# A macaron network of Mamba, mixture-of-experts and attention layers on one core: the plus one of the convolved channels' gate, made by ScalarE in place of VectorE

## The reference

```
zxbcdt = x @ in_w
z   = zxbcdt[..., :256]
xBC = zxbcdt[..., 256:256 + 512]
xp  = jnp.pad(xBC, ((0, 0), (3, 0), (0, 0)))
xBC = sum(xp[:, k:k + T, :] * conv_w[:, k] for k in range(4)) + conv_b
xBC = jax.nn.silu(xBC)
xs, Bm, Cm = xBC[..., :256], xBC[..., 256:384], xBC[..., 384:]
y = _ssd(xs * dt[..., None], dt * A, Bm, Cm)      # a scan over chunks with a carried state
y = (y + D_skip * xs) * jax.nn.silu(z)
y = y * rsqrt(mean(y * y) + 1e-05) * norm_w
return y @ out_w                                   # summed over experts with routing weights
```

## Time and profile before

| | |
|---|---|
| median of 3 runs | 2091.86 us (2088.32 to 2097.05) |
| the profiled execution | 2089.54 us, span 2087.8 us |
| mean granted TensorE clock | 0.883 |
| busy: TensorE, VectorE, ScalarE, GpSimd | 1661.6, 1350.3, 864.6, 1048.5 us |
| start of L1698, first and last of 64 | 310.2 and 982.7 us |
| L1704, 64 times | 67.6 us |
| L1809, 58 times, first and last start | 389.1 and 993.6 us |

### The profile page before, as it was taken

The page is one execution under the profiler, slowest core; times in us unless marked ns, Lnnn a source line. Parts: engine busy times, 40 slices in busy tenths (PEclk is TensorE's granted clock), DMA queues, the critical chain, the costliest instruction groups (busy, mean ns, idle before and its releaser), DMA issues. The chain is left out here.

```text
span 2087.8 us, 37246 instructions
## 1 busy us (share of the span) xinstructions
PE 1661.6 (80%) x11038; PEld 1393.8 (67%) x11039; DVE 1350.3 (65%) x3003; ACT 864.6 (41%) x1914; POOL 1048.5 (50%) x1188
## 2 busy tenths in 40 slices
PE   6889954899999999999978899528992786377773
PEld 4569941688888888888855698417881565277662
DVE  4535457899999999999655344574663565733435
ACT  2212226455555555555422122125661464334331
POOL 2135532577777777777621355244434551456552
PEclk9989956899999999999979899559995898588876
DMA  6001130000000000000050011502211410011114
GB/s 217 1 23 36 38 85 0 1 1 1 1 1 1 1 1 1 1 1 1 1 177 1 22 35 37 178 8 55 60 51 33 126 41 21 12 38 39 38 36 138
DMA packets 68555, 81.59 MB, mean 39 GB/s; under 512 B 25488, under 2 KB 40752, under 8 KB 68416
## 3 DMA queue, kind: packets, MB, share of 16 engines
q1 hardware_dynamic: 54432, 51.46, 8.0%
q0 software_dynamic: 13856, 28.40, 5.0%
q10 hardware_dynamic: 128, 0.02, 0.0%
HBM read 54.93 MB, written 24.90 MB: 38 GB/s over the span
## 5 line engine op out<-in xcount | busy, mean ns | idle before, releaser
L869 PE MATMUL ps<-w,inner_slot 128*128 x1760 | 258.7, 292 | 62.2 <-DVE y L960 37.9
L869 PEld LDWEIGHTS ps<-w,inner_slot 128*128 128x128 f32 x1760 | 229.3, 203 | 78.4 <-issue 77.6
L857 PE MATMUL ps<-gT,w_slot 128*128 128x128 f32 x1760 | 257.6, 294 | 22.9 <-ACT gT L891 19.1
L857 PEld LDWEIGHTS ps<-gT,w_slot 128*128 128x128 f32 x1760 | 235.0, 208 | 32.7 <-issue 21.3
L822 POOL DMA_INDIRECT y_rows<-y,slot_row x149 | 150.1, 1007 | 204.6 <-DVE y L954 108.0
L816 POOL DMA_INDIRECT rows_in<-xn_rows,slot_token x188 | 187.7, 998 | 125.4 <-PE ps L845 74.3
L1804 DVE SCALAR_TENSOR_TENSOR cv<-ps,cw,cv 128x1021 f32<-128x1021 f32 (+2 forms) x192 | 245.0, 1276 | 8.5 <-ACT cv L1698 5.9
L937 DVE TENSOR_TENSOR hb<-ps,b 128x512 f32<-128x512 f32 x142 | 98.2, 691 | 201.3 <-PE ps L857 116.1
L1976 POOL TENSOR_TENSOR y<-t,sz 128x256 f32<-128x256 f32 x128 | 94.4, 738 | 185.6 <-DVE t L1848 182.7
L1575 PE MATMUL ps<-xnT,win 128*128 128x512 f32 x256 | 128.7, 628 | 29.6 <-DVE cv L1804 26.2
L1624 PE MATMUL ps<-XB,LM 128*128 128x64 f32 x1024 | 142.5, 262 | 0.0
(11 more groups left out here) (298 smaller groups left out, 4201.6 us busy)
## 6 DMA issues: line engine op xcount, KB each, us to landing
w<-in_L_ffn_W SPq DMA_DIRECT2D x6, 2048.0 KB, 10.5
back<-y_rows SPq DMA_DIRECT2D x32, 256.0 KB, 5.3
xn_rows<-xn SPq DMA_DIRECT2D x24, 256.0 KB
y_rows<-y SPq DMA_DIRECT2D x71, 64.0 KB, 1.5
rows_in<-xn_rows,slot_token POOLq DMA_INDIRECT x220
y_rows<-y,slot_row POOLq DMA_INDIRECT x149
xn_rows<-rows SPq DMA_DIRECT2D x8, 256.0 KB
out_x<-x SPq DMA_DIRECT2D x8, 256.0 KB, 3.4
```

The costliest lines, as they stand in the source:

```text
L857: ins = nc.tensor.matmul(h1[:, u, b * P:(b + 1) * P], w[:, b * P:(b + 1) * P], k.gT[:, r, :], start=True, stop=True)
L869: ins = nc.tensor.matmul(py[:, q % 2, :], k.inner_slot[:, q % RING, b * P:(b + 1) * P], w_dn[:, ds(e * (FB * D) + b * D, D)], start=(b == ...
```

## The change

For the pieces inside the loop ScalarE makes the plus one too. `early_gate` is renamed `twice_sigmoid` and is called in the loop in place of `tanh_piece`; VectorE's function and its call go. The semaphores, their counts and who waits for them stay, except that ScalarE now waits for its own tanh ahead of the Identity. GpSimd's product waits for `sigmoid` as before.

```
 # ScalarE's queue
-            def early_gate(n):
+            def twice_sigmoid(n):
                 tanh_piece(n)
                 wait(act, a["tanh"], n + 1)
                 inc(A.activation(th[:, :], th[:, :], ACT.Identity, bias=k.ones[:, 0:1]), a["sigmoid"])
...
                 if ok(t - CLOSE):
                     close_unit(t - CLOSE)
                 if piece_of(t, 2) is not None:
-                    tanh_piece(piece_of(t, 2))
+                    twice_sigmoid(piece_of(t, 2))
                 if ok(t - 1):
                     square(t - 1)
...
 # VectorE's queue
-            def twice_sigmoid(n):
-                wait(dve, a["tanh"], n + 1)
-                inc(V.tensor_scalar(th[:, :], th[:, :], 1.0, None, ALU.add), a["sigmoid"])
...
                 if piece_of(t, 1) is not None:
                     tap(piece_of(t, 1), 1)
-                if piece_of(t, 2) is not None:
-                    twice_sigmoid(piece_of(t, 2))
```

More of the change, by code:

```diff
@@ L1750, in _ @@
             do(A.activation(q[:, :], u_[:, :], ACT.Ln))
-            early_gate(0)
+            twice_sigmoid(0)
             inc(A.copy(m.pickA[:, :, :], bcast(sel[:, 0, :], 2, P)), picked)
-            early_gate(1)
+            twice_sigmoid(1)
             begin(2)
@@ L1758, in _ @@
             do(A.activation(m.cd[:, :], ps_tot, ACT.Exp))
-            early_gate(2)
+            twice_sigmoid(2)
             begin(3)
@@ L1763, in _ @@
                 A.copy(m.rows[:, g * GRP * P:(g + 1) * GRP * P], k.ps[:, 6 + g % 2, :]).then_inc(rows_copied.sem, 1)
-            early_gate(3)
+            twice_sigmoid(3)
             begin(4)
@@ L1771, in _ @@
             inc(ins, weighed)
-            early_gate(4)
+            twice_sigmoid(4)
             begin(5)
@@ L1775, in _ @@
                 z_unit(u)
-            early_gate(5)
+            twice_sigmoid(5)
             for t in steps:
```

## The result

The changed kernel takes 2121.26 us, the median of 6 runs (2119.14 to 2126.11), against 2090.16 us for the kernel before in 6 runs. The ratio is 1.014, 95% interval 1.0121 to 1.0158: slower by 31.1 us (25 to 33 by the interval). The forecast was 2124 us, 32.6 us more than before.

A forecast was written before the change was run, and what follows sets the result against it. Two loops through ScalarE bound the kernel, via TensorE (10.60 us) and GpSimd (9.97, becoming 11.16). 54 periods at 0.55 (29.7 us), plus 2.4 and 0.51, sum to 32.6 us: 2124 us, 8-in-10 range 2108 to 2137.

The forecast's parts named there:

- The removed work is worth 0: VectorE, gate of z and matrices: both are released by ScalarE, so taking off 1.18 us a piece gains 0 us.
- B: Start of L1698, ScalarE's first instruction of each piece; it repeats every 10.6 us, forecast to become 11.16.
- The added work costs 1.19 us on ScalarE: ScalarE between tanh and square: the added Identity makes 0.96 us into 2.15, so 1.19 us more a piece.
- 0.63 us of it are hidden: ScalarE's spare time behind its tanh, 0.63 to 0.64 us, is used first; a steady period gains 0.55 us.
- T to B: From the start of ScalarE's tanh (L1704) to the next piece's L1698: 2.00 us before, 1.37 at least, forecast 2.56.
- B to T: From the start of L1698 to the tanh L1704, through VectorE and GpSimd's gate product: claimed to stay 8.60 us.
- the 0.2 us that I had kept for a collision: Upper bound: L1828 stretched 0.2 us by GpSimd would make it 0.75 us a period, 45 us in all.
- VectorE is the limit: Rival, faster: VectorE's load bounds the kernel, the period closes at TensorE's 10.34 us; gains 14.6 us, 2077 us; chance 0.05.
- Absorbed: Rival, no change: ScalarE's added instruction fits into spare time; 2092 us, within 5; chance 0.06.
- The whole 1.19 a piece: Rival, much slower: each piece pays all of ScalarE's added time, 57 x 1.19 = 68 us, 2160 us; chance 0.05.
- the two early periods: Pieces starting at 398.97 and 408.95 us run back to back without slack and pay in full: 2.4 us.

The follow-up runs named there:

- a quarter and a half of the columns: Kernel before with ScalarE making the plus one of 256 or 512 of 1024 columns, VectorE the rest: 1992.67 us (ratio 1.0025) and 1995.14 us (1.0032).
- the moved addition: Kernel before with VectorE's addition to x put ahead of the state update and two sums, in steps with a first tap: 1996.49 us, ratio 1.0035.
- the first experiment: Kernel before with the plus one left out on either engine for the 58 pieces in the loop: 1987.79 us, ratio 0.9991.
- the doubled work: Kernel before with a second tensor_scalar of the same size, adding zero, behind the plus one on VectorE: 2024.88 us, ratio 1.0182.

## Why the prediction was right

**The removed work is worth 0.** Right, and shown three times: the same distances from B in the trace after, no gain with the work left out, none with it moved to idle time of ScalarE.

**The added work costs 1.19 us on ScalarE.** Right: the sequence from tanh to square is 2.14 us in the changed kernel (613.23 to 615.37), 0.96 before, so 1.18.

**0.63 us of it are hidden.** Right: 0.51 us a steady period came out, for 0.55. The term was a little large, since T to B is 2.54 us and not 2.56, and since two of the kernel before's 54 periods were 0.3 us longer anyway, against one after. The experiments with a quarter and a half of the columns show the threshold in the loop. The run total of 31.1 us leaves 0.7 outside the loop's 30.4, less than the runs can tell, and the profiled pair leaves 2.7. That the forecast for the whole kernel is off by no more than 1.5 us is in part luck.

**B to T stays 8.60.** Right, in 56 of 57 periods, so neither VectorE's relief nor a new collision touched it; the 0.2 us that I had kept for a collision was not needed. It would have been needed for the moved addition, where I did not keep it.

**What was off.** VectorE's idle time before the gate is 1.63 us a period, and I had said about 1.1: I counted the instruction removed and forgot that the period itself grows by 0.5 us, which VectorE waits too. VectorE's busy time over the whole kernel fell by 61.7 us (1350.3 to 1288.6), where I had said 68, and ScalarE's rose by 64.6 (864.6 to 929.2) for 67: in part because I had added up durations, while neighbours on one engine overlap by about 0.1 us. None of this has a bearing on the time.

**The rivals.** "VectorE is the limit" fell with the first experiment, though the doubled work shows how near it is. "Absorbed" is true of the quarter of the columns in the loop, and of the Identity in its later place. "The whole 1.19 a piece" is true only where there is no slack: the two early periods, and each addition beyond the change.

The Trainium skill (SBUF — State Buffer, Who interferes with whom) says that a VectorE instruction with two SBUF inputs contends with a GpSimd instruction that reads SBUF. The traces agree: L1828 has two such inputs and takes 0.69 us, or 0.71 to 1.11 where it starts while GpSimd's `carried` or Xw is running, both of which read SBUF. How long it takes follows from what that instruction has still to run, as the last section shows.

## What to carry to other kernels

An engine that is busy 96% of a stretch need not bound it: ask what its instructions wait for and measure the distance from the start of the chain. When work moves to an idler engine, what counts is the slack at the place in its queue where it is put, here 0.63 us between the tanh and the next piece and 1.71 us seven instructions later. And a shortened loop lays bare the next limit, whose durations may change with the phase: the moved addition lost 7 us alone and won 11 together with the relief of VectorE.

## What the runs showed of the hardware

- The plus one on VectorE (L1809), 128 x 1024 in float32, took 0.69 us when GpSimd was idle at its start and 1.18 when GpSimd's product y (L1976, 0.73 us) had begun 0.10 us before it. GpSimd's own 128 x 4 addition (L1984), which began while the plus one was running, took 0.65 us, and 0.20 in the changed kernel without it.
- In all ten traces the duration of the matrices (L1828 in the kernel before) followed one rule, to within 0.01 us: it stretched by what GpSimd's `carried` or Xw had still to run when L1828 started, less 0.14 us. For L1828 (0.69 us alone) 0.17 us left made 0.71, 0.31 made 0.86, 0.42 made 0.97 and 0.56 made 1.11. The plus one, against y, follows the same rule: 0.52 left made 1.07 and 0.63 made 1.18. Where L1828 was ahead, GpSimd's Xw behind it took 1.06 us and not 0.61. GpSimd's power on 128 x 4 elements (L1986) did not stretch L1828: 0.69 us with 0.26 left. So shifting an instruction by half a microsecond against GpSimd can change its duration by 0.4 us.
- The kernel before takes 1989 us on the chip of the experiments and 2090 in the runs of the result, with a loop that is, as far as the traces show, the same. The stretch behind the last B is 1105 us in the trace of the kernel before and 1015 to 1021 in those from the chip of the experiments. The cause stays open.
